# Banded attention walked in pairs of steps, with projections three units ahead and four buffers for the transposed probabilities

## What is computed

```
q = rope(norm(x) @ Wq.T + bq); k = rope(norm(x) @ Wk.T + bk); v = norm(x) @ Wv.T + bv   # 16 heads of 64
# per head, in blocks of 128 queries; keys are those of the own and of the previous block
scores = q_block @ kcat.T * scale          # 128 x 256
scores = where(kj >= qi and kj <= qi + 128 and not before the sequence, scores, -1e30)
ctx = softmax(scores) @ vcat
x = x + merged(ctx) @ Wo.T + bo
```

## Time and profile before

| | |
|---|---|
| median of 3 runs | 1534.84 us (1534.63 to 1535.37) |
| the profiled execution, its own time | 1529.88 us |
| its span from first to last instruction | 1528.1 us |
| mean granted TensorE clock of the span | 0.918 |
| PE busy in the span | 83% |
| DVE, ACT, POOL busy in the span | 68%, 59%, 50% |
| the banded attention: first projection to last output projection | 29.8 to 782.8 us |

### The profile page before, as it was taken

One profiled execution on the slowest core, in us unless ns is written; L12 is line 12 of the kernel. 1 busy time (PEld: TensorE's weight loads), 2 busy tenths in 40 slices (PEclk: granted clock), 3 DMA queues, 4 the chain that ended last, 5 costly groups with the idle time before them and its releaser, 6 DMA issues. The chain is left out here.

```text
span 1528.1 us, 34022 instructions
## 1 busy us (share of the span) xinstructions
PE 1273.1 (83%) x9640; PEld 1004.4 (66%) x9640; DVE 1043.8 (68%) x3646; ACT 900.7 (59%) x2287; POOL 763.8 (50%) x798
## 2 busy tenths in 40 slices
PE   3999999999999999999956888629878885288892
PEld 2677766777666666766745888616765665288892
DVE  7666877878788787887854554476786788245564
ACT  2677767778686777777753444317655664144451
POOL 3676676686666857667633544400021422434452
PEclk9899999999999999999977999859989997598896
DMA  8999990000000000000031222030000000121226
GB/s 257 209 207 204 202 196 9 4 12 1 10 6 4 12 1 15 1 4 12 2 129 56 64 60 58 25 110 1 1 17 13 29 15 15 46 59 54 60 63 166
DMA packets 129396, 91.94 MB, mean 60 GB/s; under 512 B 9115, under 2 KB 122030, under 8 KB 128992
## 3 DMA queue, kind: packets, MB, share of 16 engines
q1 hardware_dynamic: 118080, 71.84, 21.7%
q0 software_dynamic: 9248, 16.94, 3.3%
q10 hardware_dynamic: 1920, 1.60, 0.3%
HBM read 30.86 MB, written 61.64 MB: 61 GB/s over the span
## 5 line engine op out<-in xcount | busy, mean ns | idle before, releaser
L923 DVE CUSTOM_DVE_ANT_0 sc<-ps,mask 128x256 f32<-128x256 f32 x512 | 196.5, 421 | 155.5 <-PE ps L730 132.8
L842 ACT ACTIVATE sc<-sc,mx 128x256 f32<-128x256 f32 x512 | 255.0, 501 | 37.2 <-DVE mx L923 33.8
L1078 POOL TENSOR_TENSOR rot<-rot,sin 128x512 f32<-128x512 f32 x128 | 177.8, 1389 | 174.0 <-DVE rot L932 173.8
L1242 POOL DMA_INDIRECT yt<-yo,xt x160 | 160.1, 1000 | 201.7 <-DVE yo L1342 172.2
L534 POOL DMA_INDIRECT xg<-r_xw,r_slot x128 | 126.6, 989 | 171.4 <-DVE r_slot L511 131.5
L850 ACT COPY pT<-pt 128x512 f32<-128x512 f32 x256 | 149.6, 584 | 93.1 <-PE pt L740 84.6
L730 PE MATMUL ps<-K,Q 64*128 64x256 f32 x1024 | 190.9, 432 | 13.4 <-DVE mx L923 13.4
L1302 ACT ACTIVATE hT<-ph,b 128x256 f32<-128x256 f32 x320 | 125.4, 476 | 87.2 <-PE ph L1265 87.2
L740 PE MATMUL pt<-ident,sc 128*128 128x128 f32 x1024 | 168.5, 287 | 0.9 <-ACT sc L842 0.6
L753 PE MATMUL po<-pT,V 128*64 128x128 f32 x2048 | 168.8, 286 | 0.0
L1283 PE MATMUL py<-w2s,hT 128*128 128x128 f32 x1280 | 164.8, 284 | 0.6 <-ACT hT L1302 0.6
(11 more groups left out here) (235 smaller groups left out, 2749.9 us busy)
## 6 DMA issues: line engine op xcount, KB each, us to landing
xg<-zeros SPq DMA_DIRECT2D x76, 520.0 KB, 9.8
xt<-xg SPq DMA_DIRECT2D x80, 130.0 KB, 2.1
got<-yt SPq DMA_DIRECT2D x32, 256.0 KB, 4.6
yt<-yo,xt POOLq DMA_INDIRECT x160, 2.2
xg<-r_xw,r_slot POOLq DMA_INDIRECT x128, 2.3
w<-in_w SPq DMA_DIRECT2D x1, 2048.0 KB, 8.5
out_x<-x SPq DMA_DIRECT2D x8, 256.0 KB, 4.2
x<-in_hidden SPq DMA_DIRECT2D x6, 256.0 KB, 8.4
```

Of the source, the lines that this page charges most:

```text
L842: nc.scalar.activation(sc[:, b, h, :], sc[:, b, h, :], ACT.Exp, scale=-1.0, bias=mx[:, b, h:h + 1], accum_out=ls[:, c % 2, b, h:h + 1]).th ...
L923: nc.vector.tensor_tensor_reduce(sc[:, b, h, :], ps[:, h, 0:2 * P], (mask0 if b == 0 else mask)[:, :], -float(HD) ** -0.5, 3e38, ALU.add, ...
L1078: nc.gpsimd.tensor_tensor(rot[:, which, :], rot[:, which, :], s.sin[:, pos(sb)], ALU.mult).then_inc(S["pool"], 1)
L1242: nc.gpsimd.indirect_dma_start(out=s.yt, out_offset=bass.IndirectOffsetOnAxis(ap=xt[:, k, r, HID:HID + 1].bitcast(U32), axis=0), in_=yo[:, ...
```

## The change

The stage is walked in pairs of steps. Index `j` (0 or 1) takes the place of `b`, and each engine's order is written anew. The scores of a pair fill both halves of the two score banks, then signal once. `AHEAD` is 3 instead of 2: q, k and v are projected three units ahead, and three units are projected before the loop. `pT` has four buffers instead of two. The routing's small matmuls write into the free half of `po` (`spare`) instead of the score banks, and all routing portions have new places. The diff, cut:

```
-        pT = m.sb("pT", [P, 2, 2, 2, P])
+        pT = m.sb("pT", [P, SB_TILES, 2, 2, P])
+        AHEAD = 3
-        ROOT, TURN, LOGITS, EXPS, COUNT = (2, 2), (3, 2), (3, 3), (4, 0), (5, 2)
-        few = ps[:, 0, 2 * P:2 * P + SB_TILES * EXPERTS]
+        STATS, ROOT, NORMALISE, TURN, READ, LOGITS = (1, 1), (2, 0), (2, 0), (2, 1), (3, 0), (3, 1)
+        SHIFT, EXPS, ORDER, CHOOSE, SUM, COUNT, SLOTS = (4, 0), (4, 0), (4, 0), (4, 1), (5, 0), (5, 1), (6, 0)
+        def spare(c):
+            return po[:, (c + 1) % 2, :]
...
# scores: both steps of a pair
+                for b in (2 * j, 2 * j + 1):
+                    for h in range(2):
+                        if not first and b == 2 * j:
+                            pe.wait_ge(S["max"], START + 2 * G - 1 + h)
...
+                        ins = nc.tensor.matmul(ps[:, h, bass.ts(b % 2, 2 * P)], Q[r, c % QBUF, b * P:(b + 1) * P],
+                                               K[r, c, b * P:(b + 2) * P], start=True, stop=True)
+                ins.then_inc(S["s"], 2)
...
# TensorE's order in a unit
+                    for j in range(2):
+                        G = SB_TILES * u + 2 * j
+                        if not past_end(G + 4):
+                            scores((c + 1) % CHUNKS, j, u + 1, G + 4)
...
+                            if j == 0:
+                                project_q(v, vc, vsb)
                             else:
+                                project_v(v, vc)
+                        if not past_end(G + 2):
+                            for b in range(2):
+                                transposes((2 * j + 2 + b) % SB_TILES, G + 2 + b)
+                        if j == 0 and not ends(sb, c):
                             project_k(v, vc, vsb)
+                        if j == 1:
                             project_out(u - 1, (c - 1) % CHUNKS, sb)
                             turn_sums(u, ends(sb, c))
...
+                        for b in range(2):
+                            values(c, 2 * j + b, u, G + b)
+                        if routed and (c, j) in (TURN, LOGITS, COUNT):
+                            pe.wait_ge(S["norm"], START + u + 1)
...
# ScalarE's order
+                        if j == 0 and not ends(sb, c):
+                            read_q(v, vc)
+                        if routed and (c, j) == READ:
+                            rt.read(act, sb - 1, spare(c - 1))
+                        if not past_end(G + 4):
+                            probabilities((c + 1) % CHUNKS, 2 * j, G + 4)
                         if not past_end(G + 2):
+                            read_pt((2 * j + 2) % SB_TILES, G + 2)
+                        if j == 0 and not ends(sb, c):
+                            read_k(v, vc)
+                        if not past_end(G + 4):
+                            probabilities((c + 1) % CHUNKS, 2 * j + 1, G + 5)
+                        if not past_end(G + 2):
+                            read_pt((2 * j + 3) % SB_TILES, G + 3)
+                        if routed and (c, j) == ROOT:
                             rt.root(act, sb - 1)
+                        if routed and (c, j) == EXPS:
                             rt.exponentials(act, sb - 1)
...
+                        if j == 1:
                             read_sums(u)
...
# VectorE's order
+                    for j in range(2):
+                        G = SB_TILES * u + 2 * j
+                        if routed and (c, j) == SHIFT:
+                            rt.shift(dve, sb - 1, few(c - 1))
+                        if routed and (c, j) == SLOTS:
+                            rt.assign(dve, sb - 1, few(c - 1))
+                            rt.slots(dve, sb - 1)
...
+                        if not past_end(G + 4):
+                            for b in range(2):
+                                maxima((c + 1) % CHUNKS, 2 * j + b, G + 4 + b)
+                        if j == 0:
                             invert(u, c)
                             normalise(u - 1, (c - 1) % CHUNKS)
                             if c == 1:
                                 add_out(sb)
+                        if j == 0 and not ends(sb, c):
+                            swap_halves(v, 0, "q_sb")
+                            times_cos(vsb, 0)
                             swap_halves(v, 1, "k_sb")
+                            times_cos(vsb, 1)
+                        if j == 1 and not ends(sb, c):
                             keep_v(v, vc)
# and behind these: STATS, NORMALISE, ORDER, CHOOSE, SUM, each at its (c, j)
...
# GpSimd: the scatters of a superblock
-                    if routed and c == 5:
+                    if routed and c == 6:
                         pool.wait_ge(s.s_zeroed, 16 * ZERO_DMAS)
-                        rt.scatter(pool, sb - 1, (0,))
...
-                        rt.scatter(pool, sb - 1, (1,))
+                        rt.scatter(pool, sb - 1, (0, 1))
                     if routed and c == 7:
                         rt.scatter(pool, sb - 1, (2, 3))
```

More of the change, by code:

```diff
@@ L672, in units @@
             u = CHUNKS * sb + c
[L673 removed]
+            return u, u + AHEAD, (c + AHEAD) % CHUNKS, (sb if c + AHEAD < CHUNKS else sb + 1)
         def ends(sb, c):
[L677 removed]
+            return isinstance(sb, int) and sb == NSB - 1 and c >= CHUNKS - AHEAD
         LAST = SB_TILES * CHUNKS * NSB - 1
@@ L783, in _ @@
             pe.wait_ge(S["xl"], START + 1)
-            for v in range(2):
+            for v in range(AHEAD):
                 project_q(v, v, 0, head=True)
@@ L789, in _ @@
                 project_v(v, v)
-            for b in range(3):
-                scores(0, b, 0, b, first=(b == 0))
-            transposes(0, 0, first=True)
+            for j in range(2):
+                scores(0, j, 0, 2 * j, first=(j == 0))
+            for b in range(2):
+                transposes(b, b, first=True)
             def turn(sb, routed):
@@ L795, in turn @@
                     u, v, vc, vsb = units(sb, c)
[L796 to L802, removed]
-                            else:
[L804 to L820, removed]
-                            project_k(v, vc, vsb)
[L822 to L826, removed]
@@ new lines, in turn @@
+                        for b in range(2):
+                            values(c, 2 * j + b, u, G + b)
+                        if routed and (c, j) in (TURN, LOGITS, COUNT):
+                            pe.wait_ge(S["norm"], START + u + 1)
+                        if routed and (c, j) == TURN:
+                            rt.turn(pe, sb - 1, spare(c))
+                        if routed and (c, j) == LOGITS:
+                            rt.logits(pe, sb - 1, few(c))
+                        if routed and (c, j) == COUNT:
+                            rt.count(pe, sb - 1, few(c))
@@ L884, in turn @@
                     u, v, vc, vsb = units(sb, c)
-                    for b in range(SB_TILES):
-                        G = SB_TILES * u + b
-                        if not past_end(G + 2):
[L888 to L893, removed]
+                    for j in range(2):
+                        G = SB_TILES * u + 2 * j
[5 more added lines that the diff above has]
+                            probabilities((c + 1) % CHUNKS, 2 * j, G + 4)
+                        if not past_end(G + 2):
+                            read_pt((2 * j + 2) % SB_TILES, G + 2)
[6 more added lines that the diff above has]
+                        if routed and (c, j) == ROOT:
                             rt.root(act, sb - 1)
-                        if routed and (c, b) == EXPS:
+                        if routed and (c, j) == EXPS:
                             rt.exponentials(act, sb - 1)
[L897 to L901, removed]
+                        if (c, j) == (3, 1) and not ends(sb, CHUNKS - 1):
                             act.wait_ge(S["k_ps"], START + CHUNKS * sb)
                             high_x(sb + 1)
-                        if b == 3:
+                        if j == 1:
                             read_sums(u)
@@ L977, in _ @@
                 keep_v(v, v)
-            for b in range(3):
+            for b in range(SB_TILES):
                 maxima(0, b, b, first=True)
@@ L1105, in unit @@
                 if spreads:
-                    spread(v - 2, (c - 2) % CHUNKS)
+                    spread(v - AHEAD, (c - AHEAD) % CHUNKS)
                 rotate(v, c, sb, 1)
             low_x(0)
-            for v in range(2):
+            for v in range(AHEAD):
                 unit(v, v, 0)
@@ L1122, in turn @@
                         take_x(sb + 1)
-                    if c == 5 and not ends(sb, CHUNKS - 1):
+                    if c == 4 and not ends(sb, CHUNKS - 1):
                         low_x(sb + 1)
```

87 lines of the change are left out of this document (40 added, 47 removed).

## The result

The changed kernel takes **1615.72 us** (median; 1612.18 to 1616.25) against 1535.11 (1534.63 to 1540.97) for the kernel before beside it: ratio 1.0518, interval 1.0492 to 1.0543, slower. The forecast was 1560, its range 1500 to 1592: the sign was right, but the loss forecast, 25 us, is less than a third of the 81 measured. The profiled execution took 1616.25, its span is 1614.2, against 1528.1 of the span before.

The account below looks back on a forecast made before the run. The DVE/POOL chain was to bound units at 10.5 us; with 13.2 of routing a superblock takes 97.2 against 93.3. Six give +23, the first -3, the last +4, start 5.6, end -4: +25, 1560 us, range 1500 to 1592.

Parts of the forecast that it names:

- the sum of the moved routing: Routing pieces in their new places cost 13.2 us a superblock (8.8 to 17), against 6.4 before.
- PE's own work: PE's matmuls in a unit fall from 10.86 to 9.8 us, bounds 9.6 to 10.86, with half the shape changes.
- the whole-array blocks: Four whole-array blocks a unit, together 5.98 us, become two, saving 0.2 twice: 5.6.
- The chain of 10.5: Scores through maxima, normalise, q rotation, spread, sums and values to next scores: 10.25 plus 0.25, 10.5 us a unit.
- rival 1: PE stays the bound: units 9.8 to 10.1, routing 6.4 as before, 1475 to 1495 us; chance 0.14.
- If the spread ends later than 7.4 us after the scores' start, PE waits: Test at turn_sums, whether it waits for POOL's rb, meant to decide between the forecast and rival 1.
- chunk 2, +4.2: ACT's late root and DVE's multiplies ahead of j = 1's maxima lengthen this unit to 14.0 to 15.5 us.
- next scores at M + 3.7: If j = 1's first maximum starts at M, maxima, keep_v, sums and values put the next scores 3.7 us later.
- rival 4: Pauses drop PE's clock in one unit of eight: 60 to 75 us on top, 1620 to 1635; chance 0.04.
- The start: One more unit projected before the loop costs 5.6 us.
- pT at 0: Four pT buffers remove a wait that nothing in the 10.86 us unit stood on: 0 us.
- Signs named: Trace signs listed beforehand: plain units 10.3 to 10.7, scores 1.06, values 1.02, rb ending PE's idle, chunk 2 over 13.5.

Follow-up runs that it names:

- run 4: Changed kernel plus unused idle matmuls (22, 9, 14 of 512 columns) ahead of turn_sums in chunks 2, 4 and 5: 1583.66 us, ratio 1.0313.
- run 9: Four chained 128x8 DVE additions, twice in chunk 0, added to the kernel with routing late, keep_v early, spread first: 1553.31 us against 1513.88.
- run 7: The kernel before the change with four pT buffers and nothing else: 1533.48 us, ratio 1.0004.
- run 5: run 3's kernel with keep_v between the two maxima of j = 1, chunk 6's mask copy behind them: 1523.78 us, ratio 0.9936.
- run 3: Changed kernel with the routing's normalise, order and accumulate all moved behind keep_v: 1538.77 us, ratio 1.0007.

## Why the prediction was right in sign and wrong in size

The main step that failed is the sum of the moved routing, "13.2 (8.8 to 17)" us a superblock: it was 25.1. The waits that it named in the chunks were there, but it put two costs at nothing: PE's clock behind the pauses (5.2 us a superblock, run 4) and the wait of small DVE operations for GpSimd (run 9). Of the 61 us between the forecast, +25, and the spans, +86, 49.5 lie in the six routed superblocks (72.9 for 23.4), 5.3 at the start and 5.9 at the end.

- **PE's own work**: pair costs were right (1.06 and 1.02). The term that failed here is the whole-array blocks, "which saves 0.2 twice: 5.6": they take 5.93. Of the saving of 0.76, 0.40 and 0.32 are in the scores and values. PE needs 10.10, inside the bounds.
- **The chain of 10.5**: the spread was taken at 1.08, as the earlier trace rows had it; it takes 0.61 here. There DVE's multiply by cos ran beside it (436.28 to 437.03), here only maxima do. The chain is then 10.0 and hidden: PE is the bound in a plain unit, as rival 1 had it, at 0.76 saved instead of 0.36. An error on the slow side. The test "If the spread ends later than 7.4 us after the scores' start, PE waits" does not follow from the prediction's own sums either: 9.8 less values 1.02 and sums 0.53 is 8.2. The spread ended 8.1 after the scores of 100.79, PE came to the sums at 8.6, and it didn't wait.
- **The routing pieces.** Forecast 13.2 us a superblock, measured 25.1 (105.92 less 8 x 10.10). By terms: chunk 2, +4.2 with the turn's 0.5, is 8.5; logits, +1.0, 2.5; order, +1.1, 3.8; accumulate and count, +1.1, 5.7; slots, scatters and the loop's turn, +4.7, 3.9 in chunks 6, 7 and 0; add_out 0.6 is right. The rule "next scores at M + 3.7" was right where the clock held: in run 4 chunk 2 is 16.3, the forecast's upper bound of 15.5 with the turn's 0.5 being 16.0. Of the 11.9 us too little, the clock is 5.2. An estimate from DVE's records puts the meetings with GpSimd at 3.7: 2.5 in the accumulate (3.25 for 0.76), 0.6 in order (0.74 for 0.19), 0.6 in chunk 2's multiplies (3.03 for 2.39). No run prices the other 3.0.
- **The missing term, the clock.** It was rival 4, at 0.04, priced at 60 to 75. Its measured price is 32 (run 4, and PE's busy time). The prediction argued against it from units with 0.57 and 1.41 us of idle PE that kept 1.00; the pauses that it forecast itself were of up to 4 us. And the trace of before held a counterexample: a unit of chunk 5, one superblock earlier than the one in the earlier trace rows, with the same pause of 1.41 (at 383.35), in which the clock fell and which took 1.7 us more than that one's 13.55:

```profile
380.40:395.61 15.21, 13.80 (x98) 10.02 (x96) 12.13 (x38) 8.58 (x24) 7.91 (x9) 0.89 0.00 0
```

The chance of rival 4 was too low, and above all a size that depends on the forecast was treated as a rival: it belongs into the sum.
- **The missing term, DVE beside GpSimd.** The accumulate was priced by its 0.76 from a unit in which GpSimd rested (it has no operation from 477.5 to 481.5). The prediction put 0.25 on the meetings of large operations and none on the small ones; run 9 shows 3.2 us for four (3.95 less 0.76).
- **The start**: 5.6 forecast, 10.9 measured. The first and second units of the three took 6.4 and 7.7 from q to q where the earlier trace rows gave 5.6, and the stretch from 29 to 61 has a clock of 0.57; the same stretch of before, 29 to 50, had 0.76. The 4 us given back at the end balance the last superblock's costs in the forecast; measured, the rest of the span is 5.9 longer; the last superblock has the late pieces too (its chunk 2 takes 18.6), but no run prices it alone.
- **pT at 0**: right alone (run 7).
- **Signs named**: scores, values, chunk 2 over 13.5 with r_rstd waiting for the root came true; plain units of 10.3 to 10.7 did not, nor rb as the main releaser, which came only once V was out of the way (run 5).

The two misses, plain units too slow (8 x 0.4 = 3.2 us a superblock) and routing too cheap (11.9), had opposite signs, so the forecast came nearer than its routing term was. And the sign was in part luck: with the plain unit right and the routing as forecast, the same sum gives 8 x 10.1 + 13.2 = 94.0 for a superblock, only 0.7 over the 93.3 of before.

What stays open: chunk 4's 0.74 for a small multiply looks like the same meeting (519.80 + 0.74 is just behind the end of GpSimd's q addition, 518.98 + 1.51), but no run isolates it; why the routed unit of chunk 3 costs 2.5 where the forecast had 1.0, of which run 5 takes 0.7 off with keep_v's place; and how much of the start is the clock's. These weren't tried.

## What to carry to other kernels

When an order is rewritten, price every moved piece by the wait of the engine that sits behind it, and follow that wait to PE: here three pieces of routing, put one place too early on an engine that was busy 65% of the span, cost 77 us; with them late, keep_v early and the spread first, 5% slower became 1.2% faster. If a forecast contains PE pauses, look at every pause of that length in the profile and at the clock behind it, not at one; if it fell once, or if no pause is as long, the clock's price goes into the sum. And take a small DVE operation's duration only from a place where GpSimd does what it will do in the new order.

## What the runs showed of the hardware

- How much small operations suffer: four additions of 128x8, chained, take 0.76 us beside a resting GpSimd and 3.95 beside a busy one (run 9). Three of the four end with a GpSimd operation, and the one that falls between two of them takes 0.17.
- After pauses of 2.2 and 5.3 us PE's values took 1.44 and 1.91 for 1.02, and its sums 1.05 for 0.53 after 3.4 and 5.3. The granted clock was 0.50 behind the longest, that is 1.2 instead of 2.4 GHz. With the pauses filled by idle matmuls it stayed at 1.00 (run 4).
- Shorter pauses cost the clock sometimes: behind the same pause of 1.8 us it fell in four of six superblocks (run 3), and behind one of 1.41 in the kernel before. The two units shown took 1.4 and 1.7 us more by it.
- GpSimd's 128x512 copy took 1.08 or 0.60, its multiply 1.51 or 1.25, by what DVE did beside it.
- Two groups of one shape side by side instead of apart saved 0.2 us in scores (1.06 for two of 0.63) and 0.16 in values (1.02 for two of 0.59), and nothing in the transposes (0.94 and 0.87, together 1.81 for 1.82). No run tells whether the change of tiling or another fixed cost of a group is what was saved.
